# Setup of a two-layer graph kernel as one unrolled walk over x, with two sum tables and loads in pieces

## The chip, the cores and the metric

The kernel runs on one core of one Trainium2 chip. The metric is device time in microseconds (us) of one execution. The profile is of one other execution, recorded by the hardware profiler; its times are counted from the span's start. Engines: PE is TensorE (matmul), PEld its weight load, DVE is VectorE, ACT is ScalarE, POOL is GpSimd, SP is SyncE, which only issues transfers and waits. A q behind an engine (SPq, ACTq, POOLq) is its sequencer.

## The reference

There are 6,250 nodes of 256 features in `x`, 100,000 edges sorted by target `dst`, and 64 attributes per edge. Two graph layers follow each other, each with a residual sum and a layer norm:

```python
x = layernorm(x + L0(x, edges, edge_attr, weights))
x = layernorm(x + L1(x, W_u, b_u, W_v, src, dst))
# L0: row, col = src, dst
msg = relu(concat(h[row], h[col], edge_attr) @ W1.T + b1) @ W2.T + b2
agg = segment_sum(msg, row)                 # summed over the source of the edge
gx, gh = agg @ W_ih.T + b_ih, h @ W_hh.T + b_hh
r, z = sigmoid(xr + hr), sigmoid(xz + hz)   # gx, gh split in three
n = tanh(xn + r * hn);  h_new = (1 - z) * n + z * h
# L1: e = leaky(s_u[src] + s_v[dst]); softmax of e over the edges of one dst, 8 heads
# out = segment_sum(x[src] * probs, dst)
```

## The kernel before

Nodes stand in NB = 49 blocks of 128. Edges stand in NT = 784 tiles of 128, in 49 groups of 16 tiles. The program has five phases that follow each other with a barrier between them.

**Setup** (`setup_phase`) prepares what layer 0 gathers. W1 is multiplied into the nodes before the edges are looked at: each block of `x` is transposed on PE (`turn_x`, L561), multiplied by both halves of W1 (`project`, L569), and gives `A_rows` (for `h[row]`, stored by SP) and the `h[col]` half. That half is split in three bfloat16 parts (`split`, L703 to L707) and scattered by POOL into the table `B_rows` (L411), at the rank of the node among the nodes that occur in `dst`. To know the ranks, the setup counts edges: one-hot matmuls and prefix sums (`prefix`, L640) give the tile in which each node's edges end (`tile_i`, L649). POOL then gathers 49 rows blocks of `dst` by that tile (L401), DVE compares and counts them in two instructions over all 49 (L685, L686), and `edges_to` is the number of edges up to each node. The number before each node is the same array shifted by one node, and is had by writing it to memory (`upto`, L466) and reading it back shifted (`edges_before`, L468). Then come the ranks (`ranked`, L699), and only then the loop over `x` (`pipeline`, 7 passes of 7 blocks). Meanwhile PE turns the weights (`jobs`, 36 transposes; `products`, 6 small matmul groups) and DVE copies them out of PSUM (L678, L681). After the loop DVE works out the tiles of layer 1 (L716 to L761), POOL gathers 8 more row blocks (L416), and DVE makes the keys of layer 1 (L764 to L776). ACT clears the whole of `B_rows` (6 stores) and the four sum tables `S` (24 stores).

**Layer 0** (`layer0_phase`) walks the 784 tiles. For each tile POOL gathers 128 rows of `A_rows` (L918, 16 tiles ahead); PE forms attribute and `h[col]` parts in PSUM (`project`); DVE adds them (L1097); ACT applies relu (L1044); PE sums the edges of one tile that share a source (L1008); ACT copies the result (`msum`, L1048); POOL adds it to one of NTAB = 4 tables in memory, tile j to table j mod 4 (L935). An adding scatter may not start before the last one into the same table has landed, so scatter j waits for scatter j-4. ACT and DVE are held to POOL by the semaphore `scatter_waited`. Twice a group SP loads the sources and places of 8 tiles, broadcast to all partitions (`srcb` 512 KB, `locb` 256 KB, L845 and L847) and 8 tiles of attributes (256 KB, L851), and once a group it stores 384 KB of `hidden` (L860) and loads a block of `x` (L856).

**Nodes** (`nodes_phase`) walks the 49 blocks: SP loads the four table blocks, `hidden` and `x`; DVE adds tables 0 and 1 (L1297), POOL tables 2 and 3 (`add_pair`, L1205); PE transposes and sums (L1234); then come the gates, the candidate (ACT), the mix (POOL: L1210, L1211), the update (DVE: L1321, L1323, L1325, L1328) and the norm's factors (POOL `deviation`: L1216 to L1221).

**Layer 1** and **output** are not touched by the change.

The order of every engine is the order in which the code is written; engines meet at semaphores only. `asked(n, ...)` in the setup is one such meeting: DVE raises `ask`, and stands still until PE has raised `answer`.

## Time and profile before

| | us |
|---|---|
| median of 3 runs | 4623.68 (4621.38 to 4627.0) |
| profiled execution, its own time | 4616.73 |
| its span | 4615.0 |
| setup, to the first load of layer 0 | 303.1 |
| layer 0, first to last scatter's start | 340.15 to 2870.52 |
| nodes, from SP's first load | 2881.43 |
| layer 1, from SP's first load | 3192.30 |

The span is the time from the first to the last instruction; the execution's own time is 1.7 us longer. Of one line of the tables below, "busy" is the union of the group's times, "mean ns" the mean of one instruction, and what stands behind "idle before" is how long the engine stood idle just before such an instruction and what ended it.

### The profile page before, as it was taken

The numbers are of one execution on the slowest core, as the hardware profiler recorded it, in microseconds if no ns is written. First come the engines' busy times: TensorE is split into PE (matmuls) and PEld (weight loads), VectorE is DVE, ScalarE is ACT, GpSimd is POOL, SyncE is SP. The second block draws the span as 40 slices with busy tenths as digits, with TensorE's granted clock in tenths as the row PEclk, the third lists the DMA queues.
The fourth block names the chain that finished last, engine by engine and source line by source line (L and its number), as shares of the span: only waits on it lengthen the run. The fifth ranks groups of instructions, "written<-read, shape, count | busy, mean of one in ns | idle before, by whom it ended". The sixth has DMA issues, their size and how long they took to land. (4 is left out here: it accounts for less than half of the span.)

```text
span 4615.0 us, 61402 instructions
## 1 busy us (share of the span) xinstructions
PE 3063.1 (66%) x13554; PEld 1879.5 (41%) x13555; DVE 2228.3 (48%) x5041; ACT 908.6 (20%) x2810; POOL 3462.2 (75%) x2931
## 2 busy tenths in 40 slices
PE   3648777777777777777877776785554555555552
PEld 2324444444444444444444443453433333333331
DVE  3543333333333333333333332897766766666667
ACT  0312222222222222222222222332000000000002
POOL 4237888888888888888888887676777777777775
PEclk7869888888889888989898888997666777777775
DMA  8767666666666666666666665666333333443342
GB/s 305 211 232 153 133 132 135 127 126 140 131 131 126 130 135 133 130 126 138 129 135 127 129 136 100 197 201 205 110 115 115 113 113 113 116 116 108 115 118 74
DMA packets 471791, 641.52 MB, mean 139 GB/s; under 512 B 173639, under 2 KB 365667, under 8 KB 467918
## 3 DMA queue, kind: packets, MB, share of 16 engines
q0 software_dynamic: 198144, 339.26, 37.2%
q1 hardware_dynamic: 246026, 254.83, 18.5%
q10 hardware_dynamic: 27588, 47.08, 3.1%
q8 instruction: 10, 0.16, 0.0%
q14 instruction: 23, 0.19, 0.0%
HBM read 448.23 MB, written 192.71 MB: 139 GB/s over the span
## 5 line engine op out<-in xcount | busy, mean ns | idle before, releaser
L935 POOL DMA_INDIRECT S<-l_msum,l_sink x784 | 1277.7, 1630 | 253.1 <-issue 216.6
L1466 POOL DMA_INDIRECT l_feats<-X_rows,l_gsrc x880 | 1038.0, 1180 | 296.6 <-issue 258.7
L918 POOL DMA_INDIRECT l_ga<-A_rows,l_gsrc x784 | 789.6, 1007 | 265.4 <-issue 168.5
L1008 PE MATMUL l_psU<-l_hid,l_same 128*128 128x257 f32 x1568 | 583.3, 457 | 540.5 <-ACT l_hid L1044 539.3
L981 PE MATMUL l_psC<-l_table,l_onehot 128*128 x4728 | 721.4, 294 | 0.0
L1048 ACT COPY l_msum<-l_psU 128x257 f32<-128x257 f32 x784 | 292.6, 373 | 1880.2 <-POOLq L934 1515.3
L1532 PE MATMUL l_psU<-l_feats,l_same 128*128 128x264 f32 x1760 | 537.8, 466 | 152.4 <-DVE l_feats L1701 134.7
L974 PE MATMUL l_psC<-W1cT,l_attrT 64*128 64x256 f32 x1576 | 620.1, 477 | 13.0 <-DMA l_table<-B_rows 13.0
L981 PEld LDWEIGHTS l_psC<-l_table,l_onehot 128*128 128x128 bf16 x4728 | 423.7, 103 | 364.4 <-issue 304.4
L1008 PEld LDWEIGHTS l_psU<-l_hid,l_same 128*128 128x128 f32 x1568 | 266.0, 213 | 674.0 <-ACT l_hid L1044 626.0
L1532 PEld LDWEIGHTS l_psU<-l_feats,l_same 128*128 128x128 f32 x1760 | 395.7, 233 | 287.8 <-issue 204.3
L1122 DVE TENSOR_TENSOR l_hidden<-l_psG,bgate 128x256 f32<-128x256 f32 x147 | 62.4, 424 | 829.5 <-PE l_psG L1023 829.5
L974 PEld LDWEIGHTS l_psC<-W1cT,l_attrT 64*128 64x128 f32 x1576 | 260.5, 206 | 267.4 <-issue 216.1
L1080 DVE TENSOR_SCALAR l_togo<-srcT,spare 128x8 f32 x98 | 28.7, 293 | 689.1 <-POOLq L934 689.1
L1044 ACT ACTIVATE l_hid<-l_ga 128x256 f32<-128x256 f32 x784 | 331.1, 422 | 0.0
L1097 DVE TENSOR_TENSOR l_ga<-l_ga,l_psC 128x256 f32<-128x256 f32 x784 | 308.4, 415 | 45.4 <-PE l_psC L981 21.3
L1611 DVE TENSOR_TENSOR acc<-acc,l_psU 128x264 f32 x440 | 188.2, 428 | 227.1 <-PE l_psU L1532 195.6
L1701 DVE TENSOR_TENSOR l_feats<-l_feats 128x1024 f32<-128x1024 f32 x220 | 263.9, 1220 | 4.4 <-DVE acc L1695 0.5
L1562 ACT ACTIVATE l_shrink<-l_psE 128x8 f32<-128x8 f32 x55 | 9.7, 177 | 951.6 <-PE l_psE L1519 951.6
L1023 PE MATMUL l_psG<-WhhT,l_xgT 128*128 128x256 f32 x588 | 196.6, 419 | 0.0
L1071 DVE TENSOR_TENSOR l_same<-l_srcb,srcT 128x1024 f32<-128x1024 f32 x99 | 120.9, 1221 | 138.2 <-PE l_psU L1008 138.2
L1023 PEld LDWEIGHTS l_psG<-WhhT,l_xgT 128*128 128x128 f32 x588 | 123.1, 209 | 20.3
(345 smaller groups left out, 3328.1 us busy)
## 6 DMA issues: line engine op xcount, KB each, us to landing
l_srcb<-src_rows SPq DMA_DIRECT2D x99, 512.0 KB, 4.5
l_locb<-lo_rows SPq DMA_DIRECT2D x55, 512.0 KB, 3.9
S<-su_zeros ACTq DMA_DIRECT2D x24, 1156.5 KB, 8.2
l_locb<-loc_rows SPq DMA_DIRECT2D x99, 256.0 KB, 5.7
nd_sums<-S SPq DMA_DIRECT2D x196, 128.5 KB, 2.2
l_attr<-in_edge_attr SPq DMA_DIRECT2D x98, 256.0 KB, 6.6
GH_rows<-l_hidden SPq DMA_DIRECT2D x49, 384.0 KB, 2.5
nd_hidden<-GH_rows SPq DMA_DIRECT2D x49, 384.0 KB, 3.1
```

Of the source, the lines that this page charges most:

```text
L918: pool.indirect_dma_start(ga[:, s, :], None, D["A"], bass.IndirectOffsetOnAxis(ap=gsrc[h][:, j % HALF:j % HALF + 1], axis=0)).then_inc(gat ...
L935: pool.indirect_dma_start(D[f"S{j % NTAB}"], bass.IndirectOffsetOnAxis(ap=sink[j // HALF][:, j % HALF:j % HALF + 1], axis=0), msum[:, j % ...
L974: nc.tensor.matmul(pc(j), attrT[j // 4 % 2][side, j % 4 // 2 * P:(j % 4 // 2 + 1) * P], K["W1cT"][side, :], start=True, stop=False)
L981: t = nc.tensor.matmul(pc(j), onehot[j // HALF % 2][:, w, j % HALF, :], flat(table[:, bass.ds(blocks[j % 4] + w, 1), n * H:(n + 1) * H]), ...
L1008: nc.tensor.matmul(psU[j % 2][:, 0:UW], same[j // HALF][:, j % HALF, :], hid[:, j % RING, :], start=True, stop=True).then_inc(agg_done, 1)
L1023: t = nc.tensor.matmul(psG[:, 0:H], xgT[:, k * P:(k + 1) * P], K["WhhT"][:, k, n * H:(n + 1) * H], start=(k == 0), stop=(k == HC - 1))
L1044: nc.scalar.activation(hid[:, j % RING, 0:H], ga[:, j % SLOTS, :], ACT.Relu).then_inc(hid_ready, 1)
L1048: nc.scalar.copy(msum[:, j % RING, :], psU[j % 2][:, 0:UW]).then_inc(msum_ready, 1)
L1097: nc.vector.tensor_tensor(ga[:, s, :], ga[:, s, :], pc(j), ALU.add).then_inc(pre_ready, 1)
L1466: pool.indirect_dma_start(feats[r][:, t, :], None, D["X1"], bass.IndirectOffsetOnAxis(ap=gsrc[r][:, t:t + 1], axis=0)).then_inc(gathered[r ...
L1532: i = nc.tensor.matmul(psU[n % 4][:, 0:XW], same[:, t, :], feats[r][:, t, :], start=(t % PAIR == 0), stop=(t % PAIR == PAIR - 1))
L1701: nc.vector.tensor_tensor(f3, f3, w3, ALU.mult).then_inc(weighted, 1)
```

## The change

The edges' first steps are reordered, so that the tiles are found from `dst` alone; `dst` shifted by one edge (`previ`) is loaded as input and not read back from memory. The loop over `x` is written out (49 blocks, no loop instruction) and starts once 8 transposes of W1 are done. Between its passes stand the steps that stood before and after the loop: PE's answers 4 to 13 at fixed blocks, DVE's at the same ones. The shift of `edges_to` is done with two matmuls against shifted unit matrices (`next_node`, `next_block`). Absent nodes get the places behind the present ones, so every row of `B_rows` is written and it is not cleared. The bfloat16 parts stand in a ring of 21 blocks (7 before), the gathered rows in one of 28. The cast of the middle part and the copies of the weights go from DVE to ACT, and the other weights are turned after the loop. POOL gathers the rows, then layer 1's rows, and scatters B last. NTAB is 2: scatter j waits for scatter j-2, and the nodes phase loads two tables and adds them in PE's accumulation. SP's loads of layer 0 are cut in pieces (2 tiles of `srcb` and `locb`, 4 tiles of `attr`), each behind one more tile's `pre_ready`.

```diff
-NTAB = 4
+NTAB = 2
@@ setup, sync
+            for b in range(NB + 3):
+                if b + UNR < NB:
+                    load_x(b + UNR)
+                if b >= 3:
+                    store_a(b - 3)
...
@@ setup, gpsimd
+            pool.wait_ge(tiles_ready, 1)
+            pool.wait_ge(dst_out, 32)
...
+                if b % UNR == 0 and b >= KEPT * UNR:
+                    pool.wait_ge(rows_done, b // UNR - KEPT + 1)
...
-            pool.wait_ge(b_clear, 16 * b_clears)
@@ setup, scalar
-            for r in range(b_table.shape[1]):
-                act.dma_start(b_table[:, r, :], zeros[:, :].bitcast(BF16)).then_inc(b_clear, 16)
...
+            def keep_mid(b):
+                act.wait_ge(rest_ready, b + 1)
+                nc.scalar.copy(parts[:, b % RING, H:2 * H], b_rest[:, b % FEW, :]).then_inc(mid_ready, 1)
@@ setup, tensor
+            for b in range(NB + 1):
+                if b < NB:
+                    turn_x(b)
+                if b >= 1:
+                    project(b - 1)
+                if b == 1:
+                    pe.wait_ge(ask, 4)
...
+                if b == SHIFT_AT:
+                    pe.wait_ge(ask, 9)
+                    nc.tensor.matmul(psR[:, 0:NB], next_node[:, :], edges_to[:, :], start=True, stop=True)
+                    nc.tensor.matmul(psK[:, 1:NB], next_block[:, :], edges_to[:, 0:NB - 1], start=True, stop=True).then_inc(answer, 1)
...
+            pe.wait_ge(a_ready, NB)
             for n, (source, _) in enumerate(jobs):
+                turn_job(FJ + n, source)
@@ setup, vector
+            def count_rows(k):
+                at, held = slice(k * UNR, (k + 1) * UNR), slice(k % KEPT * UNR, (k % KEPT + 1) * UNR)
+                dve.wait_ge(rows_in[k], 16 * UNR)
...
-            asked(5, nc.vector.tensor_tensor(before[:, :], run_to[:, :], total[:, :], ALU.subtract))
+            nc.vector.tensor_tensor(before[:, :], run_to[:, :], total[:, :], ALU.subtract).then_inc(ask, 1)
+            passes(2, 3)
+
+            dve.wait_ge(answer, 5)
@@ layer 0, sync
                     sp.wait_ge(same_ready, g * 2 + (h + 1))
-                    src_rows(h, bass.ds(g * GROUP + (GROUP + h * HALF), HALF))
+                    for k in range(HALF // PIECE):
+                        sp.wait_ge(pre_ready, g * GROUP + (h * HALF + 1 + k))
+                        src_piece(h, g * GROUP + (GROUP + h * HALF), k)
                     sp.wait_ge(attr_turned, g * 4 + 2 * (h + 1))
-                    attr_tiles(h, bass.ds(g * (GROUP * P) + (GROUP + h * HALF) * P, HALF * P))
+                    for k in range(HALF // 4):
+                        sp.wait_ge(pre_ready, g * GROUP + (h * HALF + 5 + k))
+                        attr_piece(h, g * (GROUP * P) + (GROUP + h * HALF) * P, k)
@@ nodes
-                nc.gpsimd.tensor_tensor(sums[:, 2, j, 0:H], sums[:, 2, j, 0:H], sums[:, 3, j, 0:H], ALU.add).then_inc(pair_added[1], 1)
-                nc.vector.tensor_tensor(sums[:, 0, j, 0:H], sums[:, 0, j, 0:H], sums[:, 1, j, 0:H], ALU.add).then_inc(pair_added[0], 1)
-                nc.vector.tensor_reduce(count[:, j:j + 1], sums[:, :, j, H], AX.X, ALU.add).then_inc(counted, 1)
+                nc.vector.tensor_tensor(count[:, j:j + 1], sums[:, 0, j, H:UW], sums[:, 1, j, H:UW], ALU.add).then_inc(counted, 1)
```

What follows is the order of instructions as the programs have it. First POOL in the setup, before (`x49` is 49 in a row; `su_rows<-EX_rows` is layer 1's gather):

```order
L396 AFFINE_SELECT su_under<-su_under 128x128
L401 DMA su_rows<-dst_rows,su_tile_i 128x128 x49
L403 DMA su_first_rows<-dst_rows,su_first_tile_i 50x128
L411 DMA B_rows<-su_parts,su_rank_i 6400x768 x49
L416 DMA su_rows<-EX_rows,su_xtile_i 110x384 x8
```

and the same engine after:

```order
L425 AFFINE_SELECT su_next_block<-su_next_block 128x128
L430 DMA su_first_rows<-dst_rows,su_first_tile_i 50x128
L435 DMA su_rows<-dst_rows,su_tile_i 128x128 x49
L440 DMA su_xrows<-EX_rows,su_xtile_i 110x384 x8
L446 DMA B_rows<-su_parts,su_rank_i 6400x768 x49
```

The scatters of B have moved behind layer 1's gather, to the end of POOL's setup. Next DVE, before, where it hands the counts of edges to PE (L655) and takes them back (L656):

```order
L655 TENSOR_TENSOR su_before<-su_run,su_total 112x7
L656 COPY su_total<-su_psR 112x7
L658 TENSOR_TENSOR su_rank<-su_total,su_fresh 112x7
L659 TENSOR_SCALAR su_rank_i<-su_rank 112x7
L660 TENSOR_SCALAR su_hi_i<-su_rank_i 112x7
```

and the same place after: L666 (`add_bias`), L672 (`leave_rest`) and L676 (`leave_low`) belong to the loop over `x`, the others to the chain on the edges.

```order
L763 TENSOR_TENSOR su_before<-su_run,su_total 112x7
L666 TENSOR_TENSOR su_b_rows<-su_psA,su_bias 128x256
L666 TENSOR_TENSOR su_b_rows<-su_psJ,su_bias 128x256
L672 TENSOR_TENSOR su_b_rest<-su_b_rows,su_parts 128x256
L767 COPY su_total<-su_psR 112x7
L769 TENSOR_TENSOR su_rank<-su_total,su_fresh 112x7
L770 TENSOR_SCALAR su_rank_i<-su_rank 112x7
```

Between the two steps of the chain there are now three instructions of two blocks of the loop. Last SP in layer 0, one half group after (before, this was one L845, one L847 and one L851):

```order
L974 DMA l_srcb<-src_rows 128x256
L976 DMA l_locb<-loc_rows 128x256
L974 DMA l_srcb<-src_rows 128x256
L976 DMA l_locb<-loc_rows 128x256
L974 DMA l_srcb<-src_rows 128x256
L976 DMA l_locb<-loc_rows 128x256
L974 DMA l_srcb<-src_rows 128x256
L976 DMA l_locb<-loc_rows 128x256
L984 DMA l_attr<-in_edge_attr 128x4x64 x2
```

These are the rows of the start of layer 0, where the pieces stand without waits; in the loop each pair waits for one more tile.

## Rows read from the trace of the kernel before

**Rows 1.** The page: busy times, and the two costliest groups.
```profile
PE 3063.1 (66%) x13554; PEld 1879.5 (41%) x13555; DVE 2228.3 (48%) x5041; ACT 908.6 (20%) x2810; POOL 3462.2 (75%) x2931
...
L935 POOL DMA_INDIRECT S<-l_msum,l_sink x784 | 1277.7, 1630 | 253.1 <-issue 216.6
...
L918 POOL DMA_INDIRECT l_ga<-A_rows,l_gsrc x784 | 789.6, 1007 | 265.4 <-issue 168.5
```

**Rows 2.** Stretches: length, busy of each engine, PEclk, DMA share, GB/s.
```profile
200.00:250.00 50.00, 46.69 (x143) 22.21 (x142) 35.07 (x96) 23.12 (x72) 23.16 (x24) 1.00 1.02 382
...
2900.00:3150.00 250.00, 201.31 (x927) 129.52 (x926) 226.27 (x590) 91.60 (x210) 175.91 (x296) 0.99 0.63 191
```

**Rows 3.** The setup in order of time: start, length, idle before it.
```profile
43.65 1.18 POOL L401 DMA_INDIRECT su_rows<-dst_rows,su_tile_i  x1 [40.50 <-DVE su_tile_i L649]
...
107.95 6.69 DVE L685 TENSOR_TENSOR su_rows<-su_rows,su_node 128x6272 f32<-128x6272 f32 x1 [23.51 <-DMA su_first_rows<-dst_rows,su_first_tile_i]
...
149.80 0.21 DVE L693 TENSOR_TENSOR su_any_in<-su_edges_to,su_edges_before 128x49 f32<-128x49 f32 x1 [27.96 <-DMA su_edges_before<-upto]
...
276.13 1.02 POOL L416 DMA_INDIRECT su_rows<-EX_rows,su_xtile_i  x1 [12.27 <-DVE su_xtile_i L755]
...
303.10 0.36 SPq L845 DMA_DIRECT2D l_srcb<-src_rows  x1
```

**Rows 4.** Groups in the loop over x, 190 to 247 us.
```profile
L411 POOL DMA_INDIRECT B_rows<-su_parts,su_rank_i x28 | 27.2, 970 | 31.4 <-DVE su_parts L707 31.4
L707 DVE TENSOR_TENSOR su_parts<-su_b_rest,su_parts 128x256 bf16<-128x256 f32 x27 | 11.5, 426 | 0.9
L703 DVE TENSOR_TENSOR su_b_rest<-su_b_rows,su_parts 128x256 f32<-128x256 f32 x27 | 11.2, 415 | 0.0
...
L712 DVE TENSOR_TENSOR su_b_rows<-su_psA,su_bias 128x256 f32<-128x256 f32 x16 | 6.8, 424 | 10.5 <-PE su_psA L569 10.5
```

**Rows 5.** Sum of five stretches that hold the chain outside the loop.
```profile
sum 56.90, PE 10.10 PEld 8.08 DVE 44.44 ACT 0.60 POOL 11.27; mean PE 2.02 PEld 1.62 DVE 8.89 ACT 0.12 POOL 2.25
```

**Rows 6.** PE's weights in order of time.
```profile
56.99 0.64 PE L497 MATMUL su_psJ<-ident,su_w 128*128 128x128 f32 x2
...
73.38 4.71 PE L550 MATMUL su_psJ<-su_wihT,su_w 128*128 128x384 f32 x8 [0.27 <-DVE WuvT L678]
...
81.80 1.45 PE L550 MATMUL su_psJ<-su_wihT,su_b2cols 128*128 128x384 f32 x4
```

**Rows 7.** POOL's first scatter of layer 0, in order of time.
```profile
340.15 1.64 POOL L935 DMA_INDIRECT S<-l_msum,l_sink  x1 [14.32 <-ACT l_msum L1048]
```

**Rows 8.** All scatters: min/median/max ns, and us to landing.
```profile
L935 POOL DMA_INDIRECT S<-l_msum,l_sink x784: 1559/1591/2564, 340.1 to 2870.5; - x196
...
DMA to landing us min/median/max: 3.7/4.3/8.6
```

**Rows 9.** SP and POOL in layer 0, in order of time.
```profile
1507.88 0.35 SPq L860 DMA_DIRECT2D GH_rows<-l_hidden  x1
...
1509.96 0.39 SPq L851 DMA_DIRECT2D l_attr<-in_edge_attr  x1
...
1523.61 2.36 POOL L935 DMA_INDIRECT S<-l_msum,l_sink  x1 [0.30 <-ACT l_msum L1048]
```

**Rows 10.** The one scatter that starts at 1510.85: us to landing.
```profile
DMA to landing us min/median/max: 7.6/7.6/7.6
```

**Rows 11.** POOL and DVE in one pass of the nodes phase.
```profile
3003.14 0.72 POOL L1205 TENSOR_TENSOR nd_sums<-nd_sums 128x256 f32<-128x256 f32 x1
3005.48 0.28 POOL L1216 TENSOR_TENSOR nd_rstd<-nd_moments,eps 128x1 f32<-128x1 f32 x1 [1.61 <-DVE nd_moments L1328]
...
3003.21 0.94 DVE L1321 TENSOR_TENSOR nd_tmp<-nd_tmp,nd_rz 128x256 f32<-128x256 f32 x1 [0.22 <-POOL nd_y L1211]
...
3006.09 0.42 DVE L1297 TENSOR_TENSOR nd_sums<-nd_sums 128x256 f32<-128x256 f32 x1
...
3011.33 0.19 POOL L1216 TENSOR_TENSOR nd_rstd<-nd_moments,eps 128x1 f32<-128x1 f32 x1 [1.62 <-DVE nd_moments L1328]
```

More of the change, by code:

```diff
@@ L44 @@
 PAIR = 2
+SHIFT_AT = 22
 XPACKED = XT // (PAIR * PACK)
@@ L357, in table_part @@
+            sp.wait_ge(consts, 3)
+            load_edges("src", src_in)
+            sp.dma_start(w1[:, :, :], A["W1"].rearrange("(o p) k -> p o k", p=P)).then_inc(w1_in, 16)
+            for b in range(UNR):
+                sp.dma_start(xs[:, b, :], A["x"][b * P:(b + 1) * P, :]).then_inc(x_in[b], 16)
             def table_part(n, source):
@@ L459, in _ @@
-            for t in range(NTAB // 2):
-                for piece in range(NI - 1):
-                    clear_sums(t, piece)
-            act.wait_ge(edges_ready, 1)
-            with nc.allow_non_contiguous_dma(reason="the nodes are over partitions"):
-                act.dma_start(D["upto"][0:1, :], zero[:, :]).then_inc(edges_out, 16)
-                act.dma_start(D["upto"][1:NP + 1, :].rearrange("(b p) o -> p (b o)", p=P), edges_to[:, :]).then_inc(edges_out, 16)
-                act.wait_ge(edges_out, 32)
-                act.dma_start(edges_before[:, :], D["upto"][0:NP, :].rearrange("(b p) o -> p (b o)", p=P)).then_inc(before_in, 16)
@@ L489, in _ @@
+            for n, (_, target) in enumerate(jobs):
+                keep_job(FJ + n, target)
+            for n, (_, _, target) in enumerate(products):
+                keep_job(JOBS + n, target)
+            act.wait_ge(tables_clear, 16 * NTAB * PIECES)
+            act.wait_ge(rows_out, 48)
             act.wait_ge(loc_out, 32)
@@ L528, in _ @@
-            nc.tensor.matmul(psR[0:CQ, 0:CH], ones[0:CQ, 0:CQ], before[:, :], start=False, stop=True).then_inc(answer, 1)
-            pe.wait_ge(ask, 6)
-            turn(block[:, :], psK[:, 3 * CQ:4 * CQ]).then_inc(answer, 1)
-            pe.wait_ge(ask, 7)
-            for c in range(4):
-                turn(rawf["src"][:, c, :], psR[:, c * CQ:(c + 1) * CQ])
-            for c in range(4, CH):
-                t = turn(rawf["src"][:, c, :], psK[:, (c - 4) * CQ:(c - 3) * CQ])
-            t.then_inc(answer, 1)
@@ L573, in _ @@
-            pipeline(pe, [(0, turn_x), (1, project)])
-            pe.wait_ge(ask, 9)
-            nc.tensor.matmul(psR[:, 0:2 * BT], ones[0:BT, :], spread[:, :, :].rearrange("p n b -> p (n b)"),
-                             start=True, stop=True).then_inc(answer, 1)
-            pe.wait_ge(ask, 10)
-            for c in range(XC):
-                turn(xrows[:, c, P:2 * P], (psR if c < 4 else psK)[:, c % 4 * XQ:(c % 4 + 1) * XQ])
-                turn(xrows[:, c, 2 * P:3 * P], psJ[c // 4][:, c % 4 * XQ:(c % 4 + 1) * XQ])
```

610 lines of the change are left out of this document (368 added, 242 removed).

## The prediction

> **What bounds the kernel now.** I read the page first, then a table of stretches, and then each phase's timeline or groups. In the page POOL is the busiest engine, and two of its instructions, the scatter and the gather of layer 0, are more than half of that [rows 1]. Over layer 0 the median scatter takes 1591 ns [rows 8], with about 0.3 us before each of the two for issuing (216.6 of 253.1 us over 784) [rows 1]. POOL thus never stands still there for another engine, and a tile costs what POOL costs: (2870.5 - 340.1) / 783 = 3.23 us [rows 8]. Layer 0 changes only if a scatter or gather gets longer or shorter, or if a new wait comes before it. The setup is different: in its middle no engine is the bound, but a chain. POOL first gathers at 43.65; DVE waits 23.5 us for the rows until 107.95, counts for twice 6.69 us, and waits 27.96 us until 149.80 for the shift through memory; the loop over x starts behind that. Layer 0's first load is issued at 303.10 [rows 3]. In the nodes phase DVE is busy for 226.27 of 250 us and PE for 201.31 [rows 2], but the pass is set by a circle between POOL and DVE, read from the timeline: POOL's norm factors and mix start when DVE has the moments, and DVE's update starts when POOL has the mix. One turn is 3011.33 - 3005.48 = 5.85 us [rows 11].
>
> **Setup, up to the loop.** The tiles now need `dst` only. Before, the histogram waited for the read-back of `dst` rows; now it waits for 3 loads instead of 6 and `src` and the shifted `dst` arrive beside PE's matmuls. I estimate POOL's first gather at 28 us and not 43.65, and then 3 us of transposes and 8 turns of W1. The turns cost (73.38 - 56.99) / 36 = 0.455 us each [rows 6], 4 us together. The loop would start at 37 us.
>
> **Setup, the loop.** Its three resources, per block: POOL's row gives the old pace, (27.2 + 31.4) / 28 = 2.09 us, which PE sets (46.69 of 50 us busy) [rows 4, 2]. DVE keeps add, subtract, subtract, 424 + 415 + 426 ns = 1.27 us [rows 4]; its cast goes to ACT. The chain on the edges, which stood outside the loop, is 44.4 us of DVE and 10.1 us of PE [rows 5]. For 49 blocks DVE has 62 + 44 = 106 us and PE 102 + 10 = 112. If they overlapped fully the walk would take 112. They don't: most of the chain stands before block 24, where DVE has 24 x 1.27 + 40 = 70 us against PE's 24 x 2.09 + 7 = 57, and each engine is held to the other's order by the meetings. The gather also holds here: 49 rows at about 1.27 us are 62 us, with a wait each for ring space, and from 28 us on they end near 100 us, where DVE wants the last seven; I put 5 us on that. Blocks 24 to 48 are PE's, 25 x 2.09 + 4 = 56. The sum is 75 + 56 = 131, so the loop ends at 168 us.
>
> **Setup, its end.** 28 turns at 0.455 and the products, which took 81.80 + 1.45 - 73.38 = 9.9 [rows 6], make 22.6 us: 191. Behind PE's order stands POOL: B's scatters begin at about 112 and take 49 x (0.97 + 0.3) = 62 us, until 174 and some us to land, hidden by the weights. The transfers have room, just: the old loop already ran at 382 GB/s with the share at 1.02 [rows 2]; after 112 us 9.6 MB of scatters, 6.4 MB of x and A and 7 MB of clears are 60 us at that rate. Not clearing B and two tables takes 23 MB away, which stood mostly in the gather's way. With the handover of about 5 us that lay between 298.9 and 303.10, and some us for imperfect meetings, I take 200 us for layer 0's first load, 103 us earlier. Bounds: -126 us if DVE and PE overlap fully (177), -83 if each of ten meetings costs 2 us more than I count.
>
> **Start of layer 0.** The first load of the table, on which PE waits, comes behind seven more issues at about 0.42 us: +3 us on the 37 us from 303.10 to 340.15 [rows 3, 7]; 0 to +6.
>
> **Layer 0, loads in pieces.** The mean scatter is 1630 ns and the median 1591 [rows 1, 8]: 39 ns x 784 = 31 us are long ones. They stand where SP has just issued `srcb`, as the one of 2.36 us at 1523.61 [rows 9]. In pieces of 192 KB the burst is a quarter. I take -20 us, nearer to that 31 than to nothing. The other end: if each of eight pieces a group delays a scatter by as much as one of the two bursts did, it is 31 x 3 = 94 us more.
>
> A rule speaks against this edit. Every piece here is 128 or 64 KB. The Trainium skill, DMA: Bandwidth & Descriptors, section Bandwidth (Measured), says to batch transfers to 1 MiB and that those under 64 KB are mostly descriptors; it gives 0.95 us for 64 KB against 6.15 us for 1 MB. By an estimate from its figures the pieces of half a group take about 8.6 us of the transfer engines where one load of 768 KB takes some 4.7, which would lengthen landings rather than shorten them. No trace so far shows a piece; this is why the second rival below has the chance it has.
>
> **Layer 0, two tables.** Scatter j now waits for the landing of j-2. With 3.19 us a tile when nothing is in the way, and the wait 0.3 us before the issue, a landing may take 6.1 us. The median takes 4.3, the longest 8.6 [rows 8]. The scatter at 1510.85 took 7.6 [rows 10], right behind the largest burst (SP stored `hidden` at 1507.88 and had issued three loads more by 1509.96) [rows 9]; it would have cost 1.5 us. One such a group is 49 x 1.5 = 75 us, the end on the dear side. But a piece now waits for its own tile, so the store of `hidden` stands alone, and no burst is over 384 KB where it was 1.4 MB. I take +2 us, and note that ACT and DVE may run two tiles further ahead of POOL.
>
> **Nodes.** Two loads, POOL's add (0.72 us) and DVE's add (0.42) go. DVE's add is not in the circle; what is in it is L1321, which takes 0.94 us beside POOL's add, while an instruction of the same shape (L1297) takes 0.42 [rows 11]. With the add gone I expect 0.45 us less a pass, 49 x 0.45 = 22 us. Bounds: -10 (PE, at 201.31 of 250 us, becomes the limit) and -46 (0.94 us, if DVE's sum is the limit).
>
> The timeline shows L1321 ending 0.29 us after POOL's add has ended. The Trainium skill, SBUF — State Buffer, section Who interferes with whom, says a VectorE instruction with two SBUF inputs and a GpSimd one that reads SBUF exclude each other for the whole instruction. By that rule all of 0.52 us comes back, 25 us; if the length were the instruction's own, nothing would. The trace agrees with the rule.
>
> **Sum.** -103 + 3 - 20 + 2 - 22 = -140 us. The profiled execution took 4616.7, so 4477; the median of the runs lies 7 us above it, so 4484, and I say 4485.
>
> **Rivals.**
> First, the forecast with its own range, 4450 to 4520: 75%.
> Second, layer 0 gives half or more back: pieces cost +94 where I have -20, 4599; or the tails stay and one scatter a group waits, +75, 4560. For it: the tails are there and the margin is only 1.8 us over the median. Against: the tails follow bursts, and bursts go. 12%, 4530 to 4610.
> Third, the setup gains half: the meetings between DVE and PE cost as much as the overlap brings; 50 us less, 4535. Against it stands that before, for 100 us, PE had next to nothing to do. 7%. A better overlap, 4440: 3%.
> Fourth, slower. The place is the two-table wait. If splitting makes every landing long, the tile's pace is (landing + 0.3) / 2. It passes 3.23 us at 6.2 us; the other edits bring 122 us, that is 0.156 us a tile, so the kernel becomes slower than before from a median landing of 6.5 us on. At 7.0 us it is 3.65 a tile, +330, and the time 4485 + 18 + 330 = 4833 (without the 18 us that layer 0 gave in the sum). Against it: 4.3 us now. 3%.
>
> **Range and chances.** 4440 to 4550 takes in the forecast, the third rival, and half of the second. A measurement of this kernel can tell 0.2% (9 us) from no change. Faster by more: 0.95; within: 0.02; slower: 0.03, the fourth rival.
>
> **What would show it.** Layer 0's first load at 185 to 220 us. POOL's first row gather near 28 and its B scatters from about 112. The loop at about 2.7 us a block up to block 24 and 2.1 to 2.2 behind it. The mean scatter near 1600 ns, the landing's maximum under 6.5 us, POOL's waits for scatters under 10 us in all. The nodes' pass at 5.4 us, L1321 at 0.43. Layer 1 as long as before. I am wrong if the first load of layer 0 stands after 230, if the tile's pace is over 3.27 us, or if the pass of the nodes stays at 5.8.

## The result, and the profile after

The changed kernel takes 4522.9 us (median of 4 runs, 4518.8 to 4527.5) where the kernel before takes 4623.9: a ratio of 0.978, 95% interval 0.977 to 0.980, 101 us less. Forecast were 4485 us, within 4440 to 4550; the sign and the range held, the gain was 38 us smaller than forecast. The profiled execution has a span of 4517.1 us after 4615.0. By stage, with the starts of the same instructions in both traces:

| stage | before, us | after, us | difference | forecast |
|---|---|---|---|---|
| to layer 0's first load | 303.1 | 202.0 | -101.1 | -103 |
| to the first scatter | 37.0 | 36.4 | -0.6 | +3 |
| first to last scatter | 2530.4 | 2569.1 | +38.7 | -18 |
| nodes: one pass of 49 | 5.82 | 5.18 | -0.64 | -0.45 |
| layer 1: first to last gather | 1326.7 | 1326.2 | -0.5 | 0 |

These are the setup's rows of the changed kernel in order of time (start, length, idle before it), those that answer to [rows 3]:

```profile
25.03 1.44 POOL L430 DMA_INDIRECT su_first_rows<-dst_rows,su_first_tile_i  x1 [21.10 <-DVEq L745]
34.52 0.42 DVE L666 TENSOR_TENSOR su_b_rows<-su_psA,su_bias 128x256 f32<-128x256 f32 x1 [6.06 <-PE su_psA L563]
...
117.78 1.02 POOL L446 DMA_INDIRECT B_rows<-su_parts,su_rank_i  x1 [10.84 <-DVE su_rank_i L876]
...
123.56 0.42 DVE L666 TENSOR_TENSOR su_b_rows<-su_psA,su_bias 128x256 f32<-128x256 f32 x1 [1.86 <-PE su_psA L563]
...
177.42 0.42 DVE L666 TENSOR_TENSOR su_b_rows<-su_psA,su_bias 128x256 f32<-128x256 f32 x1 [0.69 <-PE su_psA L563]
...
184.22 0.97 POOL L446 DMA_INDIRECT B_rows<-su_parts,su_rank_i  x1 [0.30 <-issue]
...
202.01 0.36 SPq L974 DMA_DIRECT2D l_srcb<-src_rows  x1
```

POOL gathers at 25.0 (28 forecast), the loop over x begins at 34.5 (37), the scatters of B at 117.8 (112) and they end at 184.2 (174). The rows at 123.56 and 177.42 are blocks 24 and 48 of the walk. Two stretches of it (PE, PEld, DVE, ACT, POOL busy; PEclk, DMA share, GB/s):

```profile
60.00:120.00 60.00, 37.61 (x81) 16.40 (x79) 40.75 (x104) 13.97 (x45) 32.84 (x33) 0.69 0.71 232
120.00:180.00 60.00, 51.93 (x166) 24.24 (x165) 36.56 (x95) 34.92 (x111) 43.98 (x44) 1.00 0.97 357
```

In the first of them nobody is near full: blocks wait for counts, counts for rows. At block 21 a second wait comes, for a place in the ring of 21: ACT may write the parts of that block only when POOL's first scatter of B (117.78) has landed.

```profile
120.43 0.40 ACT L498 CAST su_parts<-su_b_rows 128x256 bf16<-128x256 f32 x1 [8.77 <-DMA B_rows<-su_parts,su_rank_i]
```

In the second stretch the transfers are nearly full, share 0.97.

For layer 0, the page's busy times and its two groups, which answer to [rows 1], and the groups by line, which answer to [rows 8]:

```profile
PE 3121.0 (69%) x13560; PEld 1920.1 (43%) x13561; DVE 2158.0 (48%) x4919; ACT 940.8 (21%) x2901; POOL 3433.0 (76%) x2886
...
L1081 POOL DMA_INDIRECT S<-l_msum,l_sink x784 | 1278.3, 1631 | 279.0 <-issue 208.2
...
L1064 POOL DMA_INDIRECT l_ga<-A_rows,l_gsrc x784 | 801.3, 1022 | 265.2 <-issue 158.9
```

```profile
L1081 POOL DMA_INDIRECT S<-l_msum,l_sink x784: 1557/1591/2577, 238.4 to 2807.5; - x196
L1064 POOL DMA_INDIRECT l_ga<-A_rows,l_gsrc x784: 942/985/2037, 204.6 to 2770.6; - x196
```

The two groups hold the whole difference of the layer. Scatters are as long as before (1278.3 for 1277.7), so nothing of the -20 us for shorter ones came. Gathers are 11.7 us longer (801.3 for 789.6), which is no more than two profiles of the kernel before differ by (789.6 and 800.8, see below), and the idle time before the scatters grew by 25.9 us (279.0 for 253.1). What that idle time is, the list of POOL's waits (us in all, times, longest; the 0.30 us before every scatter are in it) says only half:

```profile
POOL S L1081 <- ACT l_hid L1190: 46.9, 102, 2.3
POOL S L1081 <- DMA S<-l_msum,l_sink: 3.7, 12, 0.3
```

ACT's `hid` is only a neighbour in time. A scatter waits for its own `msum` and for the landing of the scatter two before, and wherever a scatter but the first idled over 0.31 us, its `msum` had been ready for 13 us or more. That leaves the landing, which this trace pairs with no scatter (the 12 times it names one are all at the usual 0.3 us); 41 of the 102 are such waits, 16 us beyond the 0.30. The order of time fits it (POOL's scatters and SP's loads, two loads of `in_edge_attr` in one row):

```profile
2064.07 0.33 SPq L974 DMA_DIRECT2D l_srcb<-src_rows  x1
2064.57 1.58 POOL L1081 DMA_INDIRECT S<-l_msum,l_sink  x1 [0.30 <-issue]
2064.58 0.33 SPq L976 DMA_DIRECT2D l_locb<-loc_rows  x1
2065.26 0.33 SPq L974 DMA_DIRECT2D l_srcb<-src_rows  x1
2065.77 0.33 SPq L976 DMA_DIRECT2D l_locb<-loc_rows  x1
2066.83 2.19 SPq L984 DMA_DIRECT2D l_attr<-in_edge_attr  x2
2067.75 1.59 POOL L1081 DMA_INDIRECT S<-l_msum,l_sink  x1 [0.30 <-issue]
...
2072.14 1.58 POOL L1081 DMA_INDIRECT S<-l_msum,l_sink  x1 [1.51 <-issue]
```

The scatter at 2064.57 goes out into a burst of two pieces and two loads of attributes; the next but one starts 7.57 us after it, idle for 1.51 us, where two tiles take 2 x 3.18 = 6.36. It also shows why "in pieces" is not "spread": the second piece follows 1.19 us behind the first, though a tile takes 3.2. A piece waits for VectorE's add of its tile, and VectorE makes these adds in pairs, some ten tiles ahead of POOL.

In the nodes phase, rows that answer to [rows 11]:

```profile
L1358 POOL TENSOR_TENSOR nd_rstd<-nd_moments,eps x49: 189/278/444, 2838.6 to 3087.3; 128x1 f32<-128x1 f32 x49
```

```profile
L1461 DVE TENSOR_TENSOR nd_tmp<-nd_tmp,nd_rz 128x256 f32<-128x256 f32 x38 | 16.2, 425 | 13.2 <-POOL nd_y L1353 13.2
```

(3087.3 - 2838.6) / 48 = 5.18 us a pass. L1461, the old L1321, takes 425 ns on the mean of 38, where [rows 11] has 0.94.

### The profile page after: what moved, and what is told of

It is laid out like the page before. It is cut to its first block and busy times, and to the rows that moved or that the text cites. A ratio compares the mean times of both kernels' runs of the same rounds, so it can differ in the third digit from the quotient of the medians.

```text
span 4517.1 us, 64322 instructions
## 1 busy us (share of the span) xinstructions
PE 3121.0 (69%) x13560; PEld 1920.1 (43%) x13561; DVE 2158.0 (48%) x4919; ACT 940.8 (21%) x2901; POOL 3433.0 (76%) x2886
## 5 line engine op out<-in xcount | busy, mean ns | idle before, releaser
L1081 POOL DMA_INDIRECT S<-l_msum,l_sink x784 | 1278.3, 1631 | 279.0 <-issue 208.2
L1064 POOL DMA_INDIRECT l_ga<-A_rows,l_gsrc x784 | 801.3, 1022 | 265.2 <-issue 158.9
L1154 PE MATMUL l_psU<-l_hid,l_same 128*128 128x257 f32 x1568 | 599.9, 469 | 489.7 <-ACT l_hid L1190 487.0
L1127 PE MATMUL l_psC<-l_table,l_onehot 128*128 x4728 | 741.3, 299 | 0.0
L1120 PE MATMUL l_psC<-W1cT,l_attrT 64*128 64x256 f32 x1576 | 627.4, 482 | 12.9 <-DMA l_table<-B_rows 12.9
L1154 PEld LDWEIGHTS l_psU<-l_hid,l_same 128*128 128x128 f32 x1568 | 275.1, 220 | 618.3 <-ACT l_hid L1190 602.6
L1243 DVE TENSOR_TENSOR l_ga<-l_ga,l_psC 128x256 f32<-128x256 f32 x784 | 308.4, 415 | 40.7 <-PE l_psC L1127 16.7
L1169 PE MATMUL l_psG<-WhhT,l_xgT 128*128 128x256 f32 x588 | 210.8, 446 | 0.0
L1217 DVE TENSOR_TENSOR l_same<-l_srcb,srcT 128x1024 f32<-128x1024 f32 x99 | 121.1, 1224 | 123.9 <-PE l_psU L1154 123.9
L1169 PEld LDWEIGHTS l_psG<-WhhT,l_xgT 128*128 128x128 f32 x588 | 136.8, 233 | 27.5
```

Source lines behind the costliest of these rows:

```text
L1064: pool.indirect_dma_start(ga[:, s, :], None, D["A"], bass.IndirectOffsetOnAxis(ap=gsrc[h][:, j % HALF:j % HALF + 1], axis=0)).then_inc(gat ...
L1081: pool.indirect_dma_start(D[f"S{j % NTAB}"], bass.IndirectOffsetOnAxis(ap=sink[j // HALF][:, j % HALF:j % HALF + 1], axis=0), msum[:, j % ...
L1120: nc.tensor.matmul(pc(j), attrT[j // 4 % 2][side, j % 4 // 2 * P:(j % 4 // 2 + 1) * P], K["W1cT"][side, :], start=True, stop=False)
L1127: t = nc.tensor.matmul(pc(j), onehot[j // HALF % 2][:, w, j % HALF, :], flat(table[:, bass.ds(blocks[j % 4] + w, 1), n * H:(n + 1) * H]), ...
L1154: nc.tensor.matmul(psU[j % 2][:, 0:UW], same[j // HALF][:, j % HALF, :], hid[:, j % RING, :], start=True, stop=True).then_inc(agg_done, 1)
L1169: t = nc.tensor.matmul(psG[:, 0:H], xgT[:, k * P:(k + 1) * P], K["WhhT"][:, k, n * H:(n + 1) * H], start=(k == 0), stop=(k == HC - 1))
```

## Other chips

The experiments ran on three other chips, and there the kernel before is slower: 4693, 4686 to 4691 and 4659 us. So both kernels were profiled once more on the second of them (4611.7 us for the changed kernel, median of 4; 4700.1 us for the one before, a single execution).

> The changed kernel itself once more, since the four kernels of the first series ran on a chip on which the kernel before takes 4693 and not 4624 us, and on which the setup ended at 243 to 256 and layer 1 took 1358 to 1390 us. It is the anchor for this series, to be read by stages. If layer 0 and the nodes depend on POOL's instructions and waits alone, they take what they took on the first chip, 2569 and 247 us (5.14 a pass), whatever the chip; if not, the differences of the first series (2538.6 with four tables, 2631.7 with whole loads, 2611.6 and 2592.2 with an added instruction) have to be read against the new number. For the setup and layer 1 no theory says which of the two chips is the rule.

> The kernel before itself, for its stages on another chip than the first. There it took 4624, on the two others 4693 and 4686, while the changed kernel went from 4522.9 to 4611.7: it lost 89 us where before lost 62. Its layer 0 and nodes should again take 2530 and 280 us. Layer 1 of the changed kernel took 1368 on such a chip and not 1326. If before's layer 1 loses those same 42 us, its setup must have lost only 20 (layer 0's first load at 323 or so), where the changed kernel's lost 46 (248 for 202): theory A, the denser setup is the one that suffers from whatever is slower there. Theory B: before's setup loses as much, to 345 or more, and the difference stands elsewhere.

| us | to layer 0's first load | first to last scatter | pass | layer 1's gathers | span |
|---|---|---|---|---|---|
| before, first chip | 303.1 | 2530.4 | 5.82 | 1326.7 | 4615.0 |
| before, other chip | 319.8 | 2547.6 | 5.84 | 1361.7 | 4698.3 |
| changed, first chip | 202.0 | 2569.1 | 5.18 | 1326.2 | 4517.1 |
| changed, other chip | 248.1 | 2569.4 | 5.19 | 1367.9 | 4610.0 |

Layer 0 and the nodes of the changed kernel are the same to 0.5 us, so the experiments can be read by these stages. That is closer than the code explains: before's layer 0 moved by 17 us, and three kernels below that leave layer 0 as it is in the changed kernel take 2558.9, 2566.4 and 2567.8 us. A difference of under some 10 us in one profile of layer 0 thus says nothing. The setup loses 46 us after the change and 17 before: theory A of the second expectation, roughly. The ratio there is 0.983 (0.980 to 0.987). Where it goes is seen between 20 and 80 us of the changed kernel, in 40 slices (share of the DMA engines in tenths, GB/s), first on the other chip, then on the first:

```profile
DMA  9877799951223113511121111211105286996576
GB/s 267 285 188 216 171 253 288 280 187 44 82 81 105 44 44 111 195 44 44 44 74 57 44 44 44 68 63 44 44 0 175 52 230 200 406 391 185 177 126 152
```

```profile
DMA  9586799951233575498999999979999999964111
GB/s 258 185 268 233 173 256 293 287 167 57 74 131 92 173 221 146 161 236 226 409 411 233 276 403 285 263 192 370 360 383 407 404 386 323 382 199 136 49 44 44
```

On the other chip little but POOL's row gathers moves until 64 us: 1.35 MB between 42 and 63 us, 1.09 of them on POOL's queue, where the first chip moves 5.90. SP issues no load of `x` from 43 to 64 us, and the walk stands still. Before the change what may be the same lag shows only in the count of the rows, which starts at 126.78 us instead of 107.95 [rows 3]:

```profile
126.78 6.69 DVE L685 TENSOR_TENSOR su_rows<-su_rows,su_node 128x6272 f32<-128x6272 f32 x1
```

The rest of the 46 us comes later, among B's scatters, which end at 229 and not 184. What lags on those chips, and why layer 1 takes 35 to 42 us more in both kernels, stays open.

## The experiments on layer 0

**Four sum tables again.** `NTAB = 4`, and the nodes phase of before:

```diff
-NTAB = 2
+NTAB = 4
+                nc.gpsimd.tensor_tensor(sums[:, 2, j, 0:H], sums[:, 2, j, 0:H], sums[:, 3, j, 0:H], ALU.add).then_inc(pair_added[1], 1)
+                nc.vector.tensor_tensor(sums[:, 0, j, 0:H], sums[:, 0, j, 0:H], sums[:, 1, j, 0:H], ALU.add).then_inc(pair_added[0], 1)
```

> The changed kernel with four sum tables again (12 clears more in the setup, the nodes phase of before with both adds; the split loads and the new setup stay). Layer 0 went from 2530.4 us to 2569.0 between first and last scatter, where -18 was forecast. Theory A: of the 38.6 us the two tables cost 19 us in waits for landings (scatters 0, 8, 11 of a group) and 7.5 us in the last group, the rest is longer gathers. Then layer 0 takes 2542 us here, the last group 28 and not 35.6 us, the waits are gone and the nodes' pass is 5.84 us; the whole is 4522.9 - 27 + 34 = 4530. Theory B: the split loads alone lengthen layer 0; then it stays at 2565 or more, and the whole is about 4555. The setup should not take over 5 us longer for its 14 MB of clears.

Layer 0 took 2538.6 us (2542 forecast), the pass 5.83, the first load came at 256.1; the whole 4620.8 us, 0.986 of before (0.983 to 0.989).

```profile
L1081 POOL DMA_INDIRECT S<-l_msum,l_sink x784 | 1277.1, 1629 | 255.4 <-issue 212.6
L1064 POOL DMA_INDIRECT l_ga<-A_rows,l_gsrc x784 | 799.1, 1019 | 266.0 <-issue 173.7
```

The idle time is before's again, 255.4 us, and no scatter but the first idles over 0.31 us. Theory A holds: two tables cost layer 0 31 us (2569.4 - 2538.6), of which 15 are waits in the groups between and 7.5 the last group; what is left is within the spread. What they give back is less than it seems. The clears are it: the three other kernels of this chip have the first load at 243.3 to 245.2 us, so twelve stores more cost 11 to 13 us. The pass of 5.83 us is not, since a later kernel has four tables and a pass of 5.18: the pass gains from leaving the adds to PE, whatever the number of tables.

**The loads whole again.**

```diff
-        PIECE = 2
+        PIECE = 8
-                        sp.wait_ge(pre_ready, g * GROUP + (h * HALF + 1 + k))
-                for k in range(HALF // 4):
-                    attr_piece(h, edge, k)
+                attr_piece(h, edge, 0)      # 8 tiles in one
```

> The changed kernel with the loads of src_rows, loc_rows and in_edge_attr in one piece each again (512, 256 and 256 KB, the waits on pre_ready gone), two tables and the new setup kept. Theory A of the landing: the burst (hidden 384 KB, then 1 MB) holds scatters 5 and 6 of a group for 6 us or more, so that 7 and 8 wait for them: by the landings of before (medians 6.3 and 5.8 us) about 1.4 us a group, 66 us, 47 more than the 19 us of waits with the split loads; layer 0 takes 2610 us and the whole is 4565. Theory B, by which the pieces are what harms: layer 0 gets shorter than 2569, to about 2545, and the whole is 4500.

Layer 0 took 2631.7 us (2610 forecast), the whole 4667.5, 0.995 of before (0.992 to 0.997).

```profile
L1074 POOL DMA_INDIRECT S<-l_msum,l_sink x784 | 1282.0, 1635 | 352.9 <-issue 198.4
L1057 POOL DMA_INDIRECT l_ga<-A_rows,l_gsrc x784 | 788.4, 1006 | 265.9 <-issue 163.5
```

```profile
POOL S L1074 <- ACT l_hid L1183: 126.4, 115, 3.6
```

With two tables the splitting is worth 62 us, and the idle time shows it: 352.9 against 278.8 us, 74 more, while the gathers are 16 us shorter (788.4 for 804.0). The scatters themselves take 1282.0 us with whole loads and 1279.7 in pieces, so the pieces shorten them by 2 us where the prediction had 20. With four tables it is worth nothing: 2538.6 split, 2530.4 and 2547.6 whole. So the split pays only where the wait is near.

**Pieces paced by POOL.**

```diff
-                        sp.wait_ge(pre_ready, g * GROUP + (h * HALF + 1 + k))
+                        sp.wait_ge(scatter_waited, g * GROUP + (h * HALF + 1 + k))
```

> The changed kernel with the pieces of layer 0's loads paced by POOL (each waits on scatter_waited, one more per tile) instead of by VectorE's adds (pre_ready). In the trace of the changed kernel the pieces go in pairs 1.2 us apart, since VectorE's adds come in pairs, and scatters 0, 8 and 11 of a group wait 0.1 us on the mean for the landing of a scatter that met such a pair. Theory A: with the pieces 3.28 us apart, those 19 us of waits fall below 5, and layer 0 takes 2569 - 14 = 2555 us. Theory B: it is the store of hidden (384 KB in one) or any piece that lengthens the landing; then the waits stay at 15 us or more and layer 0 within 4 us of 2569.

The pairs are gone (SP in order of time):

```profile
2076.33 0.35 SPq L974 DMA_DIRECT2D l_srcb<-src_rows  x1
2076.86 0.35 SPq L976 DMA_DIRECT2D l_locb<-loc_rows  x1
2081.25 0.33 SPq L974 DMA_DIRECT2D l_srcb<-src_rows  x1
```

Layer 0 did not move: 2569.4 us, the idle time before scatters 279.7 (278.8 in the changed kernel on that chip). The waits stand mostly at scatters 1, 3, 9, 11 and 13 of a group, where the changed kernel has 0, 8 and 11. Theory B: spread out, pieces of 192 KB still bring landings over what two tables allow (18 us of waits in the groups between, where the changed kernel of that chip has 15). Whether a single piece is enough the trace can't tell, since it pairs no landing with its scatter. The whole: 4616.9 us, 0.986 (0.982 to 0.989).

**One more product on VectorE, and one more copy.** In each half group:

```diff
+                    chain.link(nc.vector.tensor_tensor(earlier[:, :, :], same[h % 2][:, :, :],
+                                                       K["before"][:, :].unsqueeze(1).to_broadcast([P, HALF, P]), ALU.mult))
```

or, in the second kernel,

```diff
+                    chain.link(nc.vector.tensor_scalar(earlier[:, :, :], same[h % 2][:, :, :], 1.0, None, ALU.mult))
```

> The changed kernel with one more VectorE instruction in each half group of layer 0: the product of same and before, 128x1024 f32 with two inputs in SBUF (L1221), is computed twice. In both traces the long scatters and gathers stand beside such a product: a fit over all of them gives 0.34 of its overlap for a scatter and 0.65 for a gather, 41 us in all, and an issue on SP beside them next to nothing. Theory A: VectorE's two-input product holds up POOL's scatters and gathers; another 98 of 1.22 us make layer 0 35 to 60 us longer (2569 -> 2605 to 2630), and the mean gather goes from 1022 to 1045 ns or more. Theory B, that of the prediction: long scatters come from SP's bursts, and VectorE has room (48% busy), so layer 0 stays within 5 us of 2569.

> The same place as the kernel with a second product, but the added instruction has one input (same times 1.0, 128x1024 f32, written to the same tile and overwritten by the product behind it). Theory A (two inputs hold POOL up): at most 10 us more than 2569 us for layer 0. A rival C, by which any work of VectorE beside a scatter holds it up: as much as the two-input product, 35 us or more. Theory B (SP's bursts): no change.

Layer 0 took 2611.6 us with the product, 42 more, and 2592.2 with the copy, 23 more (4659.3 and 4643.6 in all, 0.993 and 0.990 of before). The gathers of the two:

```profile
L1064 POOL DMA_INDIRECT l_ga<-A_rows,l_gsrc x784 | 847.0, 1080 | 265.3 <-issue 163.0
```

```profile
L1064 POOL DMA_INDIRECT l_ga<-A_rows,l_gsrc x784 | 829.4, 1058 | 266.4 <-issue 168.4
```

against 804.0 us in the changed kernel on another such chip: +43.0 and +25.4, which is the whole of what layer 0 gained in length. Theory B, the prediction's, falls: neither instruction touches a transfer. The scatters did not get longer (1278.4 and 1277.0 us), so by themselves the two kernels show the effect on gathers alone. In the changed kernel one sees the product (L1221) over a gather:

```profile
1724.69 0.99 POOL L1064 DMA_INDIRECT l_ga<-A_rows,l_gsrc  x1 [0.30 <-issue]
...
1727.84 1.22 DVE L1221 TENSOR_TENSOR l_earlier<-l_same,before 128x1024 f32<-128x1024 f32 x1
1727.88 2.04 POOL L1064 DMA_INDIRECT l_ga<-A_rows,l_gsrc  x1 [0.30 <-ACT l_hid L1190]
```

The gather that starts 0.04 us after the product takes 2.04 us instead of 0.99. It is the order that counts. Counted over all of layer 0, for gathers and scatters that start while a VectorE instruction still has over 0.1 us to run (means; "longer" is against the median gather or scatter; the product is L1217 or L1221, before L1071 or L1075):

| kernel | of POOL | VectorE runs | times | still to run, us | longer by, us |
|---|---|---|---|---|---|
| before | scatters | product | 85 | 0.45 | 0.32 |
| changed | scatters | product | 80 | 0.54 | 0.35 |
| changed | gathers | product | 47 | 0.65 | 0.52 |
| second product | gathers | the second | 43 | 1.13 | 1.00 |
| copy | gathers | the copy | 10 | 0.52 | 0.39 |
| changed | scatters | reduce, L1224 | 49 | 0.35 | -0.01 |
| changed | gathers | add from PSUM, L1243 | 112 | 0.30 | 0.00 |

POOL's instruction is longer by what the product still has to run, less 0.1 to 0.2 us. The 46 gathers of the changed kernel within which a product starts are not longer (+1 ns on the mean). So C, any work of VectorE, falls: the sum over an axis and the add from PSUM cost nothing. A stands better than its number: of the 25 us in the kernel with the copy only 4 are gathers behind the copy. Another 21 are gathers behind the products (46.0 us where the changed kernel of that series has 24.7), which the copy has moved in time.

## The experiments on the nodes and the setup

**VectorE's add back in the nodes.**

```diff
+                nc.vector.tensor_tensor(spare[:, j, :], sums[:, 0, j, 0:H], sums[:, 1, j, 0:H], ALU.add)
```

> The changed kernel with VectorE's addition of two 128x256 tiles back in the nodes phase (its result is not used), POOL's left out. The pass fell from 5.84 to 5.14 us where 5.39 was forecast. Theory A, the prediction's: VectorE's add was in the shade, POOL's alone was in the circle, and the pass stays at 5.14 to 5.2. Theory B: the circle holds VectorE's order too; the pass grows by 0.25 to 0.42 us to 5.4 to 5.56, which is the part that the forecast missed.

In the one execution measured, the pass took (3141.1 - 2882.9) / 48 = 5.38 us, 0.19 more than the 5.19 of the changed kernel there. Theory A falls, B is nearer, with a smaller price. Two groups of POOL, first of the changed kernel, then of this one:

```profile
L1352 POOL TENSOR_TENSOR nd_tmp<-nd_xs,nd_cand 128x256 f32<-128x256 f32 x39 | 29.5, 757 | 0.1
```

```profile
L1353 POOL TENSOR_TENSOR nd_tmp<-nd_xs,nd_cand 128x256 f32<-128x256 f32 x37 | 36.5, 987 | 0.1
```

VectorE's add is not in the circle, but POOL's mix is, and that is 230 ns longer with it, 987 for 757. Before the change it was 984 too. 0.19 of the 0.64 us come with VectorE's add. For the other 0.45 POOL's add is left, as forecast: alone it was not put back, but with both adds the pass is 5.83 us, with VectorE's alone 5.38, and the loads of four tables without any add leave it at 5.18 (the last kernel below).

**A longer walk before the counts, and an earlier shift.**

```diff
-SHIFT_AT = 22
+SHIFT_AT = 25
-    RING = 3 * UNR
+    RING = 24
-    KEPT = 4
+    KEPT = 3
-                passes(12 + k, 12 + k)
+                passes(10 + 2 * k, 11 + 2 * k)
```

> The changed kernel with a longer way before the counts: two blocks of x and not one stand behind each count of seven rows, the ring of B's parts holds 24 blocks and not 21, the shift stands at block 25 and not 22 (and the rows' ring holds 3 groups, not 4). In the trace of the changed kernel blocks 12 to 20 take 36 us, where PE needs 17, because each waits for seven of POOL's gathers. Theory A: these waits get filled, the walk ends about 5 blocks sooner (10 us) and layer 0's first load is issued at 192 (-10) on the first chip, as much earlier than the changed kernel on this one. Theory B: the end is set by POOL, whose B scatters begin when the ranks are known (117.8) and end at 184.2, and by the transfers; then the ranks come no earlier and the first load gains less than 3 us.

The first load was issued at 247.95 us (248.11 in the changed kernel), the whole took 4620.5 us (0.984, 0.979 to 0.989). B's scatters began at 152.97 and not 147.06: theory B. Its layer 0, not touched, took 2558.9 us. The second kernel turns it around:

```diff
-SHIFT_AT = 22
+SHIFT_AT = 19
```

> The changed kernel with the shift and the steps behind it three blocks of x earlier (19 and not 22), so that no block stands between the last count and the shift. The longer walk before the counts brought nothing (247.9 for 248.1), as if the end is set by the ranks and POOL's 49 scatters behind them. Theory A: the ranks come three blocks, some 8 us, sooner, and so does the first load of layer 0: about 240 where the changed kernel has 243 to 248, or 194 for 202 if the chip is like the first. Theory B: the walk of PE over the blocks that are left sets the end; then the three blocks only move behind the ranks and the first load stays within 3 us.

```profile
140.06 1.02 POOL L446 DMA_INDIRECT B_rows<-su_parts,su_rank_i  x1 [6.80 <-DVE su_rank_i L876]
...
238.51 0.36 SPq L974 DMA_DIRECT2D l_srcb<-src_rows  x1
```

The ranks come 7.0 us sooner and the first load 9.6 us: theory A. In all four traces with this setup (the changed kernel's two and these) the first load follows the walk's last block by 25 to 26 us, most of it the 23 us of the weights; ranks and scatters count because the ring ties the walk to them. The whole took 4593.0 us (4587 to 4603), 0.978 of before (0.974 to 0.983) on a chip on which the changed kernel had 4611.7 (4602 to 4613).

**Three tables, then four, with the early shift.**

```diff
-NTAB = 2
+NTAB = 3
+TABLE = [0, 1, 2, 0, 1, 2, 0, 2, 1, 2, 0, 1, 2, 0, 1, 2]
-                    pool.indirect_dma_start(D[f"S{j % NTAB}"],
+                    pool.indirect_dma_start(D[f"S{TABLE[j]}"],
```

> The early shift and three sum tables instead of two: of 16 scatters of a group, 14 wait for the landing of the third one before or further, and two for the second, at places where landings are short (7 and 9); the nodes phase adds the three on PE. Theory A (two tables cost waits and the last group): layer 0 falls from 2569 to about 2540, as with four tables (2538.6); the nodes' pass pays for four more matmuls, 5.16 to 5.3 us (+7 in all), and six more clears 4 us; with the early shift the whole is 25 us under the changed kernel, 0.977 of before on a chip on which the changed kernel has 0.983. Rival: PE is 86% busy in the nodes phase (172.2 of 200 us), so that the pass grows by the 0.52 us of its matmuls in full, 25 us in all, and takes back what layer 0 gives.

Layer 0 stayed at 2569.0 us; the whole took 4619.8 us (0.984, 0.979 to 0.989). Neither theory:

```profile
L1084 POOL DMA_INDIRECT S<-l_msum,l_sink x784 | 1286.3, 1641 | 258.3 <-issue 220.9
L1066 POOL DMA_INDIRECT l_ga<-A_rows,l_gsrc x784 | 816.9, 1042 | 265.4 <-issue 150.7
```

The idle time fell by 20.5 us (258.3 for 278.8), as A has it, but the gathers grew by 12.9 us and the scatters by 6.6. The count above explains it: behind a running product 59 gathers are longer by 38.8 us in all and 88 scatters by 39.3, where the changed kernel of that chip has 49 by 24.7 and 82 by 30.4. What brings them there was not tried by itself. The pass took 5.18 us: the rival falls, PE had room for four matmuls more.

```diff
-NTAB = 2
+NTAB = 4
-                nc.vector.tensor_tensor(count[:, j:j + 1], sums[:, 0, j, H:UW], sums[:, 1, j, H:UW], ALU.add).then_inc(counted, 1)
+                nc.vector.tensor_reduce(count[:, j:j + 1], sums[:, :, j, H], AX.X, ALU.add).then_inc(counted, 1)
-SHIFT_AT = 22
+SHIFT_AT = 19
```

> The early shift with four sum tables, which the nodes phase adds on PE (no add on POOL or VectorE). Three tables took the waits of POOL away (1.6 us left of 19) and the nodes' pass did not grow for the four matmuls more (5.138 us), but layer 0 stayed at 2569, since gathers and scatters got 21 us longer beside VectorE's products. Theory A: with four tables layer 0 takes 2539 us as in the kernel with four tables, the pass at most 0.1 us more than 5.16, the twelve clears more put the first load of layer 0 some 10 us later than with the early shift alone (238.5 -> 248); the whole is 15 to 20 us under the early shift, 0.975 of before. Theory B: how the products fall on gathers is chance of the order, worth 20 us either way, so that layer 0 may come out at 2560 again; then the whole equals the early shift, 0.978 to 0.980. Theory C: eight matmuls more in the nodes phase are past PE's room (166.9 of 200 us with three tables), and the pass grows by 0.3 us or more.

Layer 0 took 2541.5 us, the pass 5.18, and the first load came at 254.2, 15.7 us after the early shift's. 4557.7 us on a chip on which before takes 4658.9: 0.978 (0.976 to 0.981). Theory A in layer 0, and C falls. The 15.7 us are not the clears alone, since this chip is a third one, on which the changed kernel was not run; on one chip twelve clears cost 11 to 13. By stages it is 11 us under the early shift alone (+15.7, -26.3, -0.3), some 15 by an estimate with 12 us for the clears; against before the two ratios are equal, and the intervals of neither lie clear of the changed kernel's 0.983 (0.980 to 0.987). PE is nearly full in its nodes phase:

```profile
2850.00:3050.00 200.00, 194.05 (x1109) 151.63 (x1110) 165.86 (x469) 76.88 (x181) 115.15 (x213) 0.99 0.74 223
```

## Why the prediction came out as it did

**Setup: right in sum, not in each step.** -101.1 for -103. The first half of the walk, to block 24, took 123.6 - 34.5 = 89 us and not 75: of blocks 12 to 20 each waits for a count, and each count for seven of POOL's gathers; block 21 then waits for the ring. The sum had no term for the ring. The second half took 54 us (56 forecast), the weights 23, as said. The walk ended some 11 us late, and it was made up by the handover: layer 0's first load came about 1 us after the last weight, where 5 us and a margin were set down. B's scatters, put down as hidden, end hidden, but their start holds the walk: the early shift gained what the ranks gained. That two steps missed by 11 and 9 us and cancelled is luck, and so is the chip: on the other one the first load stands at 248 us, past the 230 from which the prediction called itself wrong.

**Layer 0 by the prediction's own sign.** It called itself wrong at a pace over 3.27 us a tile; the pace is 2569.1 / 783 = 3.28. The whole stayed within the range because the setup is 103 of the 140 us and came out.

**Loads in pieces: wrong in its cause.** -20 us rested on "they stand where SP has just issued". That reads the trace of before wrongly: of 84 scatters over 0.15 us longer than the median, 16 start within 2 us after an issue of SP, and 74 overlap a product of VectorE. The 2.36 us scatter that the prediction names [rows 9] starts 0.33 us behind one:

```profile
1523.28 1.23 DVE L1071 TENSOR_TENSOR l_same<-l_srcb,srcT 128x1024 f32<-128x1024 f32 x1 [2.09 <-PE l_psU L1008]
```

Scatters behind a running product hold 27 of the 30 us of tails. No instruction of VectorE in layer 0 was changed by the edit, and the scatters' busy time stayed at 1278 us; whole loads or pieces move it by 2. The step took a neighbour in time for a cause, and did not ask which other engine was busy beside all the long ones. The added product and copy, +42 and +23 us, confirm it for gathers; for scatters it rests on the count. The counter-argument, that small pieces lengthen the landings, did not come true either: with whole loads the waits for landings are 90 us in the groups between, with pieces 15.

**Two tables: the term was mis-sized.** +2 us were set down, 31 measured, inside the bounds of 0 to 75. The argument "no burst is over 384 KB" was half right: the bursts are smaller, but pairs of pieces, and spread-out ones too, still meet a scatter in three or four places of a group. The rows had the limit (6.1 us) and the longest landings, and no row that showed how a landing goes beside a piece. About 19 us of it are such waits in the groups between, by the idle times over 0.31 us; another 7.5 us are the last group, which has no gathers between its scatters, so that POOL waits for each landing (35.6 us against 28.0 before and with four tables). That the last 16 tiles go by another pace was not thought of. The second rival comes nearest in kind, layer 0 gives more than half back by waits for landings, but at less than half of its 75 us; the 4522.9 measured lie between the first forecast's 4520 and its 4530. Its other branch, "pieces cost +94", is wrong: whole loads would have cost 62 us more. Not asked at all was what the second pair of tables buys: some 12 us of clears, since the nodes' gain does not depend on it.

**Nodes: right in mechanism, too small.** -0.45 us a pass for L1321 is there (858 ns on the mean before, 425 after). The other 0.19 is VectorE's add, which was "not in the circle" but beside which an instruction of POOL that is in it was 0.23 us longer (one execution).

**Start of layer 0 and layer 1** as forecast, to 4 us. The sum: 57 us too hopeful in layer 0 and 2 in the setup, 12 too careful in the nodes (the stage took 276.8 us after 310.9), 4 at layer 0's start.

## What to carry to other kernels

Before a long instruction is put down to what was issued before it, list what every other engine runs beside the long ones and beside the short ones; here two rows more would have told VectorE's product from SP's burst. When a buffer or table is taken away, the wait behind it is set by the slow tail of the landing and by the stretch with another pace, the last group above all; in this kernel splitting loads paid just there. A change that takes two things away at once, here tables and adds, needs a kernel with only one of them gone before either gets the credit. And an operation that runs beside the chain is free only if it shares nothing with an engine in the chain.

## What the hardware showed

A gather of POOL, whose 128 indices lie in SBUF, takes 985 ns in the median and up to 2037 ns if it starts behind a VectorE product of two SBUF operands of 1.22 us; the 46 gathers within which a product starts keep their 985. 98 such products more, 121 us, cost the gathers 43.0 us. Ten gathers that started while a copy with one SBUF input had 0.52 us left were 0.39 us longer. The Trainium skill, SBUF — State Buffer, section Who interferes with whom, has VectorE's two-input instructions in SBUF exclude GpSimd ones that read SBUF, and copies in a two-port mode exclude GpSimd altogether: the trace agrees on both (that the copy ran in such a mode is taken from its 0.69 us at the shortest, where the product of the same size takes 1.22). It also infers that a two-input product does not hold up the making of descriptors; here gathers that start within 0.2 us behind it are 0.90 to 1.05 us longer, and the measurement decides.

One and the same kernel spends 202 or 248 us in its setup by the chip, while its layer 0 takes 2569 us on both; the denser setup lost 46 us where the looser one lost 17.
